# Batch 0 transposed by TensorE, products at the start, new hand-written orders for attention, and 128-row blocks two groups ahead

## The reference

```
xn   = layernorm(x);  q, k, v = xn Wq, xn Wk, xn Wv
x1   = x + softmax(causal(q k^T) / 16) v
xn2  = layernorm(x1)
probs = sigmoid(xn2 router^T + bias);  the best 2 of 8 experts, scores divided by their sum
out  = x1 + FFN_shared(xn2) + sum over the 2 experts of score * FFN_e(xn2)
FFN(y) = (silu(y gate) * (y up)) down, with 512 inner columns
```

## Time and profile before

| | us |
|---|---|
| median of 3 runs (lowest, highest) | 573.29 (572.55, 575.23) |
| profiled execution | 578.4 |
| its span | 576.6 |
| PE busy | 521.9 (91%) |
| DVE busy | 371.8 (64%) |
| ACT busy | 306.5 (53%) |
| POOL busy | 290.2 (50%) |
| mean granted clock of TensorE | 0.976 |

### The profile page before, as it was taken

How to read it: one execution, slowest core, us unless ns; L and a number is a source line. 1 busy time by engine, 2 the same in 40 slices (tenths; PEclk the granted TensorE clock), 3 DMA queues, 4 the chain that set the end, 5 groups by cost and what they waited for, 6 DMA issues and landing times. The chain is left out here.

```text
span 576.6 us, 14723 instructions
## 1 busy us (share of the span) xinstructions
PE 521.9 (91%) x4521; PEld 422.9 (73%) x4522; DVE 371.8 (64%) x933; ACT 306.5 (53%) x578; POOL 290.2 (50%) x236
## 2 busy tenths in 40 slices
PE   2797999798999999889799999999999999999970
PEld 1455788586777878778578888888888888888860
DVE  5579999879897978969645555455545455545440
ACT  4989778577768667544234443443444443444430
POOL 3654778557585846756014434533433343533443
PEclk9699999899999999989999999999999999999996
DMA  7988866929493948552455646565565555566523
GB/s 260 221 202 149 155 171 132 257 78 217 140 198 125 199 134 170 175 156 76 91 115 88 99 76 94 75 93 74 74 96 81 78 77 75 83 90 77 73 30 36
DMA packets 147551, 70.53 MB, mean 122 GB/s; under 512 B 122384, under 2 KB 140560, under 8 KB 147504
## 3 DMA queue, kind: packets, MB, share of 16 engines
q1 hardware_dynamic: 133904, 50.69, 42.1%
q0 software_dynamic: 13600, 19.22, 19.0%
HBM read 19.48 MB, written 23.54 MB: 75 GB/s over the span
## 5 line engine op out<-in xcount | busy, mean ns | idle before, releaser
L1767 PE MATMUL bank<-xn2t,w 128*128 128x256 f16 x1728 | 197.1, 273 | 2.9 <-DMA xn2t<-rows 2.5
L1767 PEld LDWEIGHTS bank<-xn2t,w 128*128 (+1 forms) x1728 | 168.5, 98 | 26.5 <-issue 2.8
L712 POOL DMA_INDIRECT out<-p,wm x56 | 89.2, 1593 | 115.2 <-DMA out<-p,wm 44.6
L1336 DVE SCALAR_TENSOR_TENSOR th<-th,bank 128x512 f32<-128x512 f32 x88 | 60.1, 683 | 75.3 <-ACT th L806 75.2
L1781 PE MATMUL bank<-w,h 128*128 (+1 forms) x840 | 98.5, 273 | 2.1 <-DVE z L1268 2.0
L1781 PEld LDWEIGHTS bank<-w,h 128*128 128x128 f16 x840 | 81.5, 98 | 13.5 <-DVE z L1268 3.5
L762 ACT ACTIVATE h<-th 128x512 f16<-128x512 f32 x72 | 45.2, 628 | 85.3 <-DVE th L1345 83.5
L806 ACT ACTIVATE th<-bank 128x512 f32<-128x512 f32 x88 | 52.5, 596 | 58.4 <-PE bank L1767 58.2
L1171 DVE TENSOR_TENSOR h<-th,h 128x512 f16<-128x512 f32 x72 | 49.8, 691 | 41.1 <-ACT h L762 41.1
L601 POOL TENSOR_TENSOR w<-wst,w 128x768 f16<-128x768 f32 x36 | 59.1, 1642 | 31.4 <-ACT w L762 31.1
L625 POOL DMA_INDIRECT rows<-xrow,sidx x56 | 57.4, 1026 | 27.5 <-DVE sidx L1328 15.9
(11 more groups left out here) (159 smaller groups left out, 728.3 us busy)
## 6 DMA issues: line engine op xcount, KB each, us to landing
wst<-w_all SPq DMA_DIRECT2D x36, 384.0 KB, 3.6
x<-x SPq DMA_DIRECT2D x8, 512.0 KB, 5.6
out<-x SPq DMA_DIRECT2D x8, 512.0 KB, 4.6
rows<-xrow POOLq DMA_DIRECT2D x1, 1192.5 KB, 7.3
rows<-xrow,sidx POOLq DMA_INDIRECT x56, 4.3
out<-p,wm POOLq DMA_INDIRECT x56, 4.0
wm<-rows SPq DMA_DIRECT2D x28, 9.0 KB, 1.8
xn2t<-rows SPq DMA_TRANSPOSE x28, 3.6
```

Of the source, the lines that this page charges most:

```text
L712: cc.indirect_dma_start(out, bass.IndirectOffsetOnAxis(ap=index, axis=0), part, None, compute_op=ALU.add).then_inc(y_out, 16)
L1336: d.scalar_tensor_tensor(out=tb, in0=tb, scalar=1.0, in1=G[half][:, :], op0=ALU.add, op1=ALU.mult).then_inc(f_sg, 1)
L1767: ins = mm(dst, w_ap(j, ws, m * MAT + k * I + (2 * half + i) * P, P), moving(ms * KD + k), start=(cnt == 0), stop=(cnt == 3 * KD - 1))
```

## The change

1. Batch 0's normalised rows are no longer copied to `xnrow` and transposed by a DMA. ACT normalises two of the four blocks of rows, DVE the other two (`first_xn_normalise`), PE multiplies them in float32 by an identity `ident32` into two PSUM banks (`first_transposes`), and ACT and DVE write hi and lo parts from there to `xnt`. POOL builds `ident32` among its constants.
2. PE runs 10 products of zeros before its first real product and 9 behind the transposes (`warm_up`).
3. The hand-written orders of batches 0 to 2 and of `iteration(i)` are new on all five streams; `iteration` now ends with batch 6, and batch 7 and the last shared tiles have a written-out order.
4. In stage 2 the single blocks run one group further ahead: group i has the down product of single i+2 and the gate and up products of single i+3. Groups 12 and 13 have no gate and up products of a single, and group 13 no down product of one. The first loads are reordered (transposed rows first, `aux` later), the table of singles is computed earlier, and the down product of pair 0 comes before that of single 0.

The core of the diff (orders are cut to PE and SP in `iteration` and to the ends that the prediction speaks of):

```diff
+            def warm_up(n):
+
+                pe.wait_ge(c_dve, 2)
+                for i in range(n):
+                    mm(G[0][:, :], h_odd[:, 0:P], h_odd[:, 0:512], start=True, stop=True)
...
+            def first_transposes(h):
+
+                pe.wait_ge((xn_put, xn0_dve)[h], 1)
+                for n in (2 * h, 2 * h + 1):
+                    for k in range(KD):
+                        ins = mm(XN_BANK[k][:, n * P:(n + 1) * P], xn32[:, n * D + k * P:n * D + (k + 1) * P],
+                                 ident32, start=True, stop=True)
+                ins.then_inc(xn0_mm, 1)
...
+            def first_xn_normalise():
+
+                dve.wait_ge(shift1, 1)
+                for i in (2, 3):
+                    ins = d.tensor_scalar(xn32[:, i * D:(i + 1) * D], x1[:, i * D:(i + 1) * D], rstd[0][:, i:i + 1],
+                                          nmr[:, i:i + 1], ALU.mult, ALU.add)
+                ins.then_inc(xn0_dve, 1)
+
+            def first_xn_low(k):
+
+                dve.wait_ge(xn0_hi, k + 1)
+                low(xnt4[:, :, KD + k, :], bank3(XN_BANK[k]), xnt4[:, :, k, :]).then_inc(xn0_lo, 1)
...
+            def first_xn_high(k):
+
+                act.wait_ge(xn0_mm, 2)
+                copy(xnt4[:, :, k, :], bank3(XN_BANK[k])).then_inc(xn0_hi, 1)
...
+            warm_up(10)
             wm_product()
+            first_transposes(0)
+            first_transposes(1)
+            warm_up(9)
             t_product(0, 0, 2)
             v_product(0, 0, 2)
             scores(0, 0, 4)
...
             def iteration(i):
 
-                scores(i, 0, 3)
+                scores(i, 0, 2)
                 shared_gate_up(2 * i - 4, 0)
+                scores(i, 2, 3)
+                shared_gate_up(2 * i - 4, 1)
                 scores(i, 3, 4)
-                shared_gate_up(2 * i - 4, 1)
                 shared_gate_up(2 * i - 3, 0)
                 shared_gate_up(2 * i - 3, 1)
                 logits(i - 1)
-                pv(i, 0, 2)
-                shared_down(2 * i - 4, 0, 1)
-                pv(i, 2, 3)
-                shared_down(2 * i - 4, 1, 2)
+                pv(i, 0, 1)
+                shared_down(2 * i - 4, 0, 2)
+                pv(i, 1, 2)
                 t_product(i + 1, 0, 1)
-                pv(i, 3, 4)
                 shared_down(2 * i - 3, 0, 2)
+                pv(i, 2, 4)
                 t_product(i + 1, 1, 2)
...
             def iteration(i):
 
                 w_load(4 * i + 1)
-                xn2_transpose(i - 1, 0)
                 w_load(4 * i + 2)
                 p_transpose(i, 0)
+                xn2_transpose(i - 1, 0)
                 xn2_transpose(i - 1, 1)
+                xn_transpose(i + 1)
                 p_transpose(i, 1)
                 p_transpose(i, 2)
-                xn_transpose(i + 1)
+                p_transpose(i, 3)
                 w_load(4 * i + 3)
-                p_transpose(i, 3)
...
+            def last_adds():
+
+                i = GROUPS - 1
+                y_add(2 * i - 1, 1, 8 * i + 8, GROUP_ADDS * i)
+                y_add(2 * i, 2, 8 * i + 8, GROUP_ADDS * i + 32)
+                pool.wait_ge(ax_in[3], 8 * GROUPS)
+                pool.wait_ge(y_out, GROUP_ADDS * i + 64)
...
-            group(GROUPS - 2, 0)
-            group(GROUPS - 1, 1, last=True)
+            group(GROUPS - 2, 0, single=False)
+            group(GROUPS - 1, 1, single=False, down_single=False)
             last_down()
```

More of the change, by code:

```diff
@@ L517, in _ @@
             first_group()
-            group(1, 1)
-            with sp.Fori(2, GROUPS - 2, 2) as i:
+            second_group()
+            group(2, 0)
+            group(3, 1)
+            with sp.Fori(4, GROUPS - 4, 2) as i:
                 for s in range(2):
                     group(i + s, s)
-            group(GROUPS - 2, 0, last=True)
+            group(GROUPS - 4, 0)
+            group(GROUPS - 3, 1, single=False)
+            group(GROUPS - 2, 0, single=False)
             sp.wait_ge(y_out, 32 * PAIRS + 16 * SINGLES)
@@ L1047, in iteration @@
                 v_high(i + 1, 1)
+                w_high(4 * i + 4)
                 xn2_normalise(i, 0)
-            for i in range(FILL, B):
+            for i in range(FILL, B - 1):
                 iteration(i)
+            exp_of(7, 0)
+            p_high(7, 0)
+            exp_of(7, 1)
+            xn2_high(6, 0)
+            p_high(7, 1)
+            xn2_normalise(6, 1)
+            tanh(10, 0)
+            xn2_high(6, 1)
+            exp_of(7, 2)
+            p_high(7, 2)
+            tanh(10, 1)
+            exp_of(7, 3)
+            p_high(7, 3)
+            split_h(10, 0)
+            split_h(10, 1)
+            tanh(11, 0)
+            tanh(11, 1)
+            logits_exp(6)
+            w_scale(29)
+            w_high(29)
+            w_scale(30)
+            w_high(30)
+            split_h(11, 0)
+            split_h(11, 1)
             tanh(12, 0)
+            w_scale(31)
+            xn2_normalise(7, 0)
             xn2_high(7, 0)
+            split_h(12, 0)
             xn2_normalise(7, 1)
@@ L1155, in _ @@
                     group(i + s, s)
[L1156 to L1157 removed]
+            group(GROUPS - 2, 0, single=False)
+            group(GROUPS - 1, 1, single=False, copy_single=False)
             last_copy()
@@ L1654, in iteration @@
                 shift_2(i)
-                v_low(i + 1, 0)
-            for i in range(FILL, B):
+            for i in range(FILL, B - 1):
                 iteration(i)
+            row_numbers(5)
+            row_max(7, 0)
+            minus_max(7, 0)
+            row_max(7, 1)
+            minus_max(7, 1)
+            add_shared(9)
+            p_low(7, 0)
+            v_low(7, 1)
+            row_max(7, 2)
+            minus_max(7, 2)
+            p_low(7, 1)
+            row_max(7, 3)
+            ffn_gate(10, 0)
@@ L1712, in ffn, with group @@
                 ffn_low(t, half)
-            def group(i, last=False):
+            def group(i, single=True):
                 t = 2 * i + SHARED
@@ L1717, in group @@
                     ffn(t, half)
-                if not last:
-                    single_h(i + 2)
+                if single:
+                    single_h(i + 3)
                 for half in range(2):
@@ L1730, in _ @@
             ffn(SHARED + 1, 1)
-            with dve.Fori(1, GROUPS - 1) as i:
+            ffn(SHARED + 2, 0)
+            single_h(3)
+            ffn(SHARED + 2, 1)
+            ffn(SHARED + 3, 0)
+            single_h(4)
+            ffn(SHARED + 3, 1)
+            with dve.Fori(2, GROUPS - 2) as i:
                 group(i)
-            group(GROUPS - 1, last=True)
+            group(GROUPS - 2, single=False)
+            group(GROUPS - 1, single=False)
         @block.tensor
@@ L2090, in group @@
                 gate_up(t, 1, j0, pair_moving(0), False)
-                single_down(i + 1, 1 - par)
-                if not last:
-                    single_gate_up(i + 2, par, 8 * i + (32 - 8 * par))
+                if down_single:
+                    single_down(i + 2, par)
+                if single:
+                    single_gate_up(i + 3, 1 - par, 8 * i + (32 + 8 * par))
                 j1 = expert(2 * i + 1)
```

741 lines of the change are left out of this document (435 added, 306 removed).

## The result

The changed kernel takes 579.39 us (median of 11 runs, 573.25 to 582.60) where the kernel before takes 573.83 us on the same chip: a ratio of 1.0069, 95% interval 1.0038 to 1.0100. It is 0.7% slower, and 24 us above the forecast of 555.2.

A forecast was written before the change was run, and what follows sets the result against it. Products on PE were taken to bound the routed experts, and nearly the attention and shared-expert stage. Gains of 4.3 + 1.5 + 4.6 + 1.5 + 1.7 + 4.5 = 18.1 us took 573.3 to 555.2 us, range 548 to 564.5.

The forecast's parts named there:

- Start of the routed experts: Start of stage 2: covering a 1.2 us wait for a single's h and 0.5 for rows gains 1.7 us, bounds 0 and 1.7.
- Rival F: POOL's adds are late for another reason (late aux load or result-buffer slot), middle loses 2 us a batch: near 573, chance 0.03.
- Start, 4.3: Kernel start: PE transposes and zero products bring the first t product to 14.4 us; 4.3 us gained at batch 1.
- Batches 0 to 2, 1.5: First attention batches: part of 3.3 us of named waits goes, gaining 1.5 us, bounds -1 and 3.3.
- The three named waits: Batches 0 to 2: low part of P (1.5 us), prefix(0) (1.0) and sums of prefix(1) (0.8), 3.3 us together, addressed.
- Batches 3 to 6, 4.6: Middle batches: of 9.0 us idle and slow products, 4.4 stay, so 4.6 us gained, bounds 8 and -4.
- The wait for z: Middle batches: PE's logits wait, 0.7 us three times, was to vanish because DVE now reads the logits first.
- the hold that the forecast moved: Middle batches: DVE's 2 us hold beside POOL's weight subtraction moves behind the logits, priced at nothing, up to 2 us uncovered.
- Batch 7, 1.5: Batch 7 and change of stage: of 7.0 us idle and about 1.5 slow products, 1.5 us gained, between 0 and 4.
- Tail, 4.5: After PE's end: the last single's add moves out of the final adds, gaining 4.5 us, bounds 3.5 and 4.5.
- B's doubt about the middle: Only the ends give; each middle wait goes over into another because DVE is near 88%: 562.8 us, chance 0.24.
- E's wait for P's block 1: SP's xn transpose ahead of P's blocks 1 to 3 delays block 1 every batch: 580.6 us, chance 0.04.

The follow-up runs named there:

- after_again: The changed kernel repeated unaltered, on a chip with unexplained engine pauses, against the kernel before: 595.4 us, ratio 1.0173.
- after_third: The changed kernel repeated unaltered, on another chip with pauses, against the kernel before: 599.5 us, ratio 1.0205.
- after_fourth: The changed kernel repeated unaltered, on a chip without pauses, against the kernel before: 580.30 us, ratio 1.0047.
- old1_new2: Stage 1 as before, stage 2 (routed experts) as changed, against the kernel before, chip with pauses: 597.83 us, ratio 1.0188.
- fix_both: Changed kernel with single 2's aux behind single 3's rows, later groups' aux last and h transposes earlier: ratio to before 0.9989 with pauses, 0.9851 repeated without.
- rows_ahead: fix_both with first two groups' rows and h transposes also ahead of aux loads that wait for adds: 585.82 us, ratio to before 0.9948, with pauses.
- rows_ahead_again: rows_ahead repeated on a chip without pauses, against the kernel before: 566.24 us, ratio 0.9802.
- spread: fix_both with POOL's scatters of batches 1 to 5 in runs of one or two: 579.29 us, ratio to before 1.0020, chip without pauses.
- fix_first: Changed kernel with only single 2's aux load moved behind single 3's rows: 595.81 us, ratio to the kernel before 1.0162, chip with pauses.
- rows_ahead_no_zeros: rows_ahead without the 19 products of zeros: 587.98 us, ratio to the kernel before 1.0009, chip with pauses.
- before_again: The kernel before repeated unaltered, for its trace, on a chip without pauses: 577.41 us, beside 577.54 us for the kernel before there.
- start_only: The kernel before with only TensorE's batch 0 transposes and the zero products, all orders old: 591.43 us, ratio to before 1.0114, with pauses.

## Why the prediction was wrong, step by step

**Start of the routed experts: the step that failed.** The forecast gave this stage 1.7 us, from two waits that the new order covers, and said that only its ends could give something. It lost 17.8. The two old waits did go, but the forecast put no term for new waits in SP's queue. The change's loads were read as "transposed rows first, aux later", which is true of the first four blocks only: the aux of single 2 moved ahead of the transpose of its h, and stayed ahead of single 3's rows. A single's aux waits for an add, and adds trail PE far: single 0's down product began at 284.71, and SP was let go behind its add at 300.33. The down product of pair 0, priced as cover for the wait for h, is also what put single 0's add later, and with singles one group further ahead PE needs what stands behind the aux sooner.

In the changed kernel, the wait and the slow products behind it are 8.5 + (5.30 - 2.76) + (3.08 - 2.78) = 11.3 us; twelve smaller waits of 0.21 to 0.62 us for the transposed h and behind it ("issue") from 356 to 521 us add 5.3. The last product adds 1.25, but by chance: it took 1.51 us in after_again. That is 17.9, and 1.7 us of old waits went, so some 1.6 of the 17.8 have no row of their own. The size varies: in after_again, after_third, after_fourth and old1_new2 the long wait is 6.9 to 7.4 us, and the way to the last product 294.5 to 299.7 us against 282.9 and 284.2 in the two traces of the kernel before, a loss of 10 to 17 us. That SP's order is the cause is shown by fix_both and rows_ahead, which change nothing else. Rival F named "a late aux load" and gave it 0.03 and the wrong place and price: it put the harm on POOL's adds, not on the rows queued behind the aux.

**Start, 4.3: right, in part by luck.** The first t product at 14.64 (14.4 forecast) in 2.76 us, batch 1's first product at 24.77 (24.9), 4.5 us earlier than in the earlier trace rows:

```profile
6.78 1.99 PE L1933 MATMUL bank<-v 128*128 128x256 f32 x8 [0.99 <-DMA v<-wk_t]
...
14.64 2.76 PE L2066 MATMUL bank<-xnt,wm 128*128 128x512 f16 x12 [1.09 <-DVE xnt L1299]
...
24.77 1.47 PE L2066 MATMUL bank<-w,wm 128*128 128x512 f16 x6 [1.19 <-DMA w<-xnrow]
```

Two errors in it nearly cancel. The transposes were priced at half of wm's product because both were taken as eight products; the eight rows of wm's are four products in the code, and the transposes are eight of half the width in sixteen rows, the same work: 2.05 us, not 1.7. And wm's product takes 1.99 us in nine of the fifteen runs with zero products (up to 3.42 in the others) and 3.40 to 3.78 in the five without, in this trace and in that of before both at a granted clock of 1.00. The first ten therefore help it in most runs, as the Trainium skill's rule has it (TensorE: Matmul & The Clock Gate, "What's actually happening"), by which an idle array runs at 1.2 GHz until it has been busy: here the durations agree with the rule and the clock column doesn't.

**Batches 0 to 2, 1.5: wrong sign.** Batch 3's scores begin at 83.78 instead of 86.85, 3.1 us of the 4.5 that the start gained, so these batches lost 1.4. The three named waits became others, P's block 1 and the logits' z among them:

```profile
31.93 0.83 PE L2041 MATMUL bank<-v,ptr 128*128 128x256 f16 x6 [1.45 <-DMA ptr<-w]
...
70.68 1.49 PE L1979 MATMUL bank<-w,h 128*128 128x256 f16 x12 [1.05 <-DVE z L1405]
```

**Batches 3 to 6, 4.6: the sum right, two readings wrong.** They run from 83.78 to 204.14, 120.4 us against 125.0, as forecast. The P waits are gone. The wait for z is not: 0.63 us in each. The row sums now take 0.15 us; DVE's 2 us hold beside POOL's subtraction went to the operation that is beside it now. The Trainium skill (SBUF — State Buffer, "Who interferes with whom") says that a VectorE instruction with two inputs in SBUF contends with a GpSimd instruction that reads SBUF, and the trace agrees in all four iterations: in 3, 4 and 5 the small operation takes 2.23 us instead of 0.15, and in iteration 6 a low part of h takes 2.86 instead of 0.68.

```profile
94.90 2.23 DVE L1324 SCALAR_TENSOR_TENSOR nmr<-mv,rstd 128x4 f32<-128x4 f32 x1
...
95.44 1.66 POOL L659 TENSOR_TENSOR w<-wst,w 128x768 f16<-128x768 f32 x1
...
99.31 0.18 DVE L1405 SCALAR_TENSOR_TENSOR z<-bank,biases 128x32 f32<-128x32 f32 x1
...
185.93 2.86 DVE L1299 TENSOR_TENSOR h<-th,h 128x512 f16<-128x512 f32 x1
...
186.58 1.65 POOL L659 TENSOR_TENSOR w<-wst,w 128x768 f16<-128x768 f32 x1
```

The hold ends at 97.13, and DVE then works without a gap until it reads the logits at 99.31, 0.8 us after PE has finished them. So the hold that the forecast moved "behind the logits" and priced at nothing stands ahead of them, and DVE's lateness fits it. No run takes the hold away alone, so that it causes the wait is not shown.

A wait that the forecast did not name came in batch 3: its last product is followed by 2.10 us of waiting for the low part of the next t (0.65 in batch 4). The high part was late because ACT stood for a weight piece that comes first in its list, so one entry held what stood behind it, as in SP's queue:

```profile
113.24 0.84 ACT L844 ACTIVATE wst<-wst 128x768 f32<-128x768 f32 x1 [2.33 <-DMA wst<-w_all]
...
115.35 0.51 PE L2111 MATMUL bank<-xnt,tt 128*128 128x128 f16 x6 [2.10 <-DVE tt L1299]
```

The four batches took 31.6, 30.1, 29.3 and 29.3 us, about 30.1 each as forecast only in the mean.

**Batch 7, 1.5: too much.** 0.4 us (64.8 against 65.2). The wait for pair 0's rows fell from 2.50 us to 0.47, but PE still waited 1.44 us for the second norm's rows (2.10 before), and 1.38, 0.60 and 0.82 for x (0.85 before).

**Tail, 4.5: right.** From PE's end 9.7 us (10.7 forecast) against 15.1, a gain of 5.5, of which the slow last product accounts for 1.25: from its start the gain is 4.2. There is no single's add among the last eight:

```profile
558.76 1.55 POOL L780 DMA_INDIRECT out<-p,wm  x1 [2.97 <-DMA out<-p,wm]
...
573.53 1.55 POOL L780 DMA_INDIRECT out<-p,wm  x1 [0.31 <-issue]
```

**The sum.** 4.5 - 1.4 + 4.6 + 0.4 - 17.8 + 5.5 = -4.2 us of span. Without the stage 2 term it would be 13.6 gained, 2.4%; rows_ahead_again, which repairs that stage, measured 2.0%. Of the rivals, B's doubt about the middle was right for batches 0 to 2 alone; E's wait for P's block 1 appeared in batches 0 to 2 and in spread, and was at most 0.27 us elsewhere in the changed kernel's trace.

## What to carry to other kernels

When a load moves in a queue, ask of each entry what it waits for and list what is queued behind it, also in a stage where the bound engine is 98% busy; an entry that waits for the far end of the pipeline (here an add) belongs behind everything the near end needs. Moving work one stage further ahead brings forward when its loads are needed, but not the completions that stand ahead of them in the queue: check these first. A removed wait proves nothing until the total moves: fix_first removed 8.5 us of wait and made its stage only 3.8 us shorter, for the next entry had the same fault.

## What the hardware showed that was not expected

On some chips ACT stood still for up to 9.3 us and DVE for up to 5.6 us (rows_ahead and rows_ahead_no_zeros), in part together, with no releaser in the records; the same program on other chips had none, and its stage 1 was 13 to 17.5 us longer with them (after_again and after_third against after_fourth and the first chip). The change's gain in stage 1 is absent on these chips; that the pauses took it is argued from where they lie. The product of float32 parts ran in 1.99 us in the changed kernel and in 3.78 us in before_again, at the same granted clock of 1.00, most often short where PE had been busy before it. And a 128x4 operation of DVE that takes 0.15 us took 2.23 us beside one subtraction of POOL and 4.88 us beside two (start_only).
